# Attention walks of a graph network: the next chunk's small products a quarter chunk earlier, and the gathers' waits at the beginnings of the groups

## The reference, cut to what matters

```python
h = einsum(x, W)                        # per node, 8 heads
e = leaky_relu(a_src[src] + a_dst[dst], 0.2)
e_max = segment_max(e, dst)             # over the edges of a destination
e_exp = exp(e - e_max[dst])
out = segment_sum(h[src] * e_exp, dst) / segment_sum(e_exp, dst)
```

## Time and profile before

| | |
|---|---|
| median of three runs | 6823.27 us |
| profiled execution: its time | 6820.69 us |
| profiled execution: its span | 6818.9 us |
| TensorE matmul / weight load busy | 4848.6 us (71%) / 3393.1 us (50%) |
| VectorE, ScalarE, GpSimd busy | 3942.6 us (58%), 2371.9 us (35%), 3022.1 us (44%) |
| granted TensorE clock, mean | 0.808 |
| messages L903 (all four walks) | 416 instructions of about 1247 ns |
| gathers L780 (all four walks) | 1664 instructions of about 0.98 us |

### The profile page before, as it was taken

How to read it: one execution, slowest core, us unless ns; L and a number is a source line. 1 busy time by engine, 2 the same in 40 slices (tenths; PEclk the granted TensorE clock), 3 DMA queues, 4 the chain that set the end, 5 groups by cost and what they waited for, 6 DMA issues and landing times. The chain is left out here.

```text
span 6818.9 us, 79751 instructions
## 1 busy us (share of the span) xinstructions
PE 4848.6 (71%) x19231; PEld 3393.1 (50%) x19232; DVE 3942.6 (58%) x8585; ACT 2371.9 (35%) x5719; POOL 3022.1 (44%) x2932
## 2 busy tenths in 40 slices
PE   2777659537775937776577738888899555477999
PEld 2455436325553725544355534444587333355777
DVE  4566733446667246665466657666424788787333
ACT  1343312124443224443244424544221122275333
POOL 2666432446662046662666536666000677553000
PEclk8777859767887968887688858888899665687999
DMA  4455424234442034443444511111001899873000
GB/s 117 151 167 166 106 66 127 86 103 143 152 153 61 1 105 152 143 152 90 144 142 152 133 41 29 31 31 26 21 9 51 315 379 381 295 220 118 10 14 23
DMA packets 543457, 819.09 MB, mean 120 GB/s; under 512 B 87966, under 2 KB 421967, under 8 KB 542839
## 3 DMA queue, kind: packets, MB, share of 16 engines
q1 hardware_dynamic: 396388, 432.93, 19.6%
q0 software_dynamic: 140832, 376.78, 19.3%
q10 hardware_dynamic: 5907, 5.92, 0.3%
HBM read 658.06 MB, written 157.71 MB: 120 GB/s over the span
## 5 line engine op out<-in xcount | busy, mean ns | idle before, releaser
L780 POOL DMA_INDIRECT l_edges_stage<-l_h_rows,src_t x832 | 822.6, 989 | 592.7 <-issue 222.5
L2507 POOL DMA_INDIRECT l_edge_kv<-l_kv_rows,src_t x416 | 477.0, 1147 | 651.1 <-POOLq L2414 517.5
L1093 PE MATMUL l_edges_ps_sum<-l_edges_msg,l_edges_hot 128*128 128x264 f32 x1664 | 591.0, 499 | 213.4 <-DVE l_attn_acc L922 134.1
L2935 POOL DMA_INDIRECT l_gate_edges_srow<-l_gate_src_rows,l_gate_edges_idx x512 | 487.1, 951 | 325.7 <-issue 140.8
L2560 PE MATMUL l_edge_ps_q<-l_q_q,l_edge_hot 128*128 x832 | 352.5, 598 | 287.6 <-issue 201.7
L3071 PE MATMUL l_gate_edges_ps<-l_gate_edges_wide,l_gate_edges_hot_lo 128*128 128x500 f32 x1024 | 492.8, 627 | 83.3 <-issue 57.3
L780 POOL DMA_INDIRECT l2a_edges_stage<-l2a_h_rows,src_t x416 | 408.2, 981 | 295.6 <-issue 126.5
L1093 PEld LDWEIGHTS l_edges_ps_sum<-l_edges_msg,l_edges_hot 128*128 128x128 f32 x1664 | 357.6, 239 | 362.9 <-DVE l_attn_acc L922 207.8
L780 POOL DMA_INDIRECT l2b_edges_stage<-l2b_h_rows,src_t x416 | 408.6, 982 | 288.6 <-issue 126.2
L2560 PEld LDWEIGHTS l_edge_ps_q<-l_q_q,l_edge_hot 128*128 128x128 f32 x832 | 238.4, 300 | 401.8 <-issue 353.9
L922 DVE TENSOR_TENSOR l_attn_acc<-l_attn_acc,l_edges_ps_sum 128x264 f32 x832 | 349.8, 420 | 84.5 <-DVE l_attn_acc L922 20.3
(11 more groups left out here) (784 smaller groups left out, 10870.1 us busy)
## 6 DMA issues: line engine op xcount, KB each, us to landing
l_edge_e<-e_rows SPq DMA_DIRECT2D x416, 128.0 KB
l_val_rows<-l_edge_vj SPq DMA_DIRECT2D x104, 512.0 KB
l_agg_stage<-l_val_rows SPq DMA_DIRECT2D x52, 1024.0 KB, 5.5
l_edges_rel_b<-rel_rows SPq DMA_DIRECT2D x52, 512.0 KB
l_edges_ea<-in_edge_attr SPq DMA_DIRECT2D x48, 512.0 KB
e_rows<-l_edges_e_s SPq DMA_DIRECT2D x48, 512.0 KB
l_experts_w<-in_L_ffn_w SPq DMA_DIRECT2D x32, 512.0 KB, 5.0
l_gate_edges_lo_b<-l_gate_edges_lo_rows SPq DMA_DIRECT2D x64, 256.0 KB
```

Source lines behind the costliest of these rows:

```text
L780: nc.gpsimd.indirect_dma_start(out=stage[:, c % SL, u, :], out_offset=None, in_=h_rows, in_offset=bass.IndirectOffsetOnAxis(ap=K.src_t[:, ...
L1093: nc.tensor.matmul(ps_sum[u][:], hot[:, g, u, :], msg[:, g % 2, u, :], start=True, stop=True).then_inc(summed, 1)
L2507: nc.gpsimd.indirect_dma_start(out=kv[:, m, u, :], out_offset=None, in_=kv_rows, in_offset=bass.IndirectOffsetOnAxis(ap=K.src_t[:, n * EB ...
L2935: nc.gpsimd.indirect_dma_start(out=srow[:, n % 4, u, :], out_offset=None, in_=src_rows, in_offset=bass.IndirectOffsetOnAxis(ap=idx[:, n * ...
```

## The change

On VectorE the chain of the next chunk starts before the first message: `rescale`, `logits`, `weigh` 0, `tile_ends` with no adds in it, `weigh` 1, `tile_tops` with the adds of group 0, `weigh` 2, `edge_maxima` with the adds of group 1, `weigh` 3, the adds of group 2, `exponents`, `nodes_hot`, the adds of group 3. TensorE's small products each move ahead by one `scatter`, ScalarE's `rescaling` moves to behind group 1, and GpSimd waits for the small products at the beginnings of the groups, beside the wait for the message. Nothing is computed otherwise.

```diff
@@ gpsimd
                         if c >= SL:
                             pool.wait_ge(msg_built, NG4 * (c - SL) + g + 1)
+                            signal = (lg_turned, ends_placed, inits_made, max_turned)[g]
+                            pool.wait_ge(signal, c - SL + 2)
                         for u in range(g * GR, (g + 1) * GR):
-                            if c >= SL and u % GR == GR // 2:
-                                signal = (lg_turned, ends_placed, inits_made, max_turned)[g]
-                                pool.wait_ge(signal, c - SL + 2)
@@ vector, chunk(c, j, i, after)
-                    weigh(c, i, 0)
                     blks = block_ids(nc, mybir.EngineType.DVE, K, c)
                     rescale(c, blks[0])
                     if after >= 1:
                         logits(c + 1, j, i + 1)
-                    for g, step in enumerate((tile_ends, tile_tops, edge_maxima)):
+                    weigh(c, i, 0)
+                    if after >= 1:
+                        tile_ends(c + 1, i + 1, lambda u: None)
+                    for g, step in ((0, tile_tops), (1, edge_maxima)):
                         weigh(c, i, g + 1)
                         if after >= 1:
                             step(c + 1, i + 1, adds(c, g, blks))
...
+                    weigh(c, i, 3)
+                    for u in range(GR):
+                        adds(c, 2, blks)(u)
                     if after >= 1:
                         exponents(c + 1, i + 1)
                     if after >= 2:
                         nodes_hot(c + 2, j, i + 2)
                     for u in range(GR):
-                        adds(c, GR - 1, blks)(u)
+                        adds(c, 3, blks)(u)
@@ scalar, chunk
                         last_maxima(c, m, g)
+                        if after and g == 1:
+                            rescaling(c + 1, 1 - m)
...
                     if after:
-                        rescaling(c + 1, 1 - m)
                         edges_hot(c + 1, 0)
@@ tensor, chunk
+                    if after >= 1:
+                        turn_logits(c + 1, 1 - m)
                     scatter(c, 0)
                     if after >= 1:
-                        turn_logits(c + 1, 1 - m)
+                        place_ends(c + 1)
                     if after >= 2:
                         turn_attr(c, m, 0, j * 16 + 16 * (m + 1))
                     scatter(c, 1)
                     if after >= 1:
-                        place_ends(c + 1)
+                        place_tops(c + 1)
                     if after >= 2:
                         attr_terms(c, 0)
                     scatter(c, 2)
                     if after >= 1:
-                        place_tops(c + 1)
+                        place_f(c + 1)
+                        turn_maxima(c + 1)
                     if after >= 2:
                         turn_attr(c, m, 1, None)
-                    scatter(c, 3, 0, GR // 2)
-                    if after >= 1:
-                        place_f(c + 1)
-                        turn_maxima(c + 1)
-                    scatter(c, 3, GR // 2)
+                    scatter(c, 3)
```

More of the change, by code:

```diff
@@ L1107, in chunk @@
                     if after >= 1:
-                        place_tops(c + 1)
+                        place_f(c + 1)
+                        turn_maxima(c + 1)
                     if after >= 2:
                         turn_attr(c, m, 1, None)
-                    scatter(c, 3, 0, GR // 2)
-                    if after >= 1:
-                        place_f(c + 1)
-                        turn_maxima(c + 1)
-                    scatter(c, 3, GR // 2)
+                    scatter(c, 3)
                     if after >= 2:
                         blks = block_ids(nc, mybir.EngineType.PE, K, c + 2)
-                    if after >= 2:
                         attr_terms(c, 1)
```

## The result

The changed kernel takes **7072.4 us** (median of 4 runs, 7061.9 to 7079.0), the kernel before 6824.3 on the same chip: ratio **1.036** (95% interval 1.035 to 1.038). The forecast was 6890, the range 6740 to 6990. The direction was right; the loss is 248 us and not 70. The profiled execution took 7067.5 us, its span is 7065.6.

The account below looks back on a forecast made before the run. A ring through GpSimd was taken as the bound, `place_tops` and `expand` showing only after GpSimd pauses. Terms gave +0.60 us a chunk, +55 us in 92 chunks, plus 11 and 4: 6820.7 + 70 = 6890 us, range 6740 to 6990.

Parts of the forecast that it names:

- rival A: TensorE's old order, not gathers, delays `place_tops` and `expand`; in the new order both show when they end: 6620 us, chance 0.10.
- (a): GpSimd's wait at group 0: restart 2.64 us behind the reduction, now also needing message 0; +0.70 us a chunk.
- (b): GpSimd's wait at group 1: `ends_placed` is there in time, the stop of 0.52 us goes; -0.30 us a chunk.
- (c): GpSimd's wait for the message of group 0, 0.68 us in some chunks, joins the group 0 wait; -0.15 us a chunk.
- (d): GpSimd's wait at group 2: `place_tops` ends before the stop but is held as before; +0.25 us a chunk.
- (e): Way from `inits_made` to `expand`, with one more `scatter` and a message: late by 0 to 2.3 us, taken as +0.10 a chunk.
- Rival D: TensorE becomes late, its clock at 0.50 from `inits_made` to `expand`: 6988 us, chance 0.13.
- (f): GpSimd's wait for `max_turned` at group 3: there 4.1 to 5.2 us after `inits_made`, needed after 5.3; costs nothing.
- (g): VectorE's turn of the loop: the load of block numbers now in the open before `rescale`; +0.9 us in 12 chunks, +11 us.
- (h): Last chunks of a walk, without gathers: the load of block numbers in the open, +1 us each, +4 us in all.
- B: Results are held, but not longer than some 3 us, so `place_tops` comes out by itself: 6775 us, chance 0.16.
- C: The change doesn't move the chain, since `logits` waits for `expanded` before and after: 6823 us, chance 0.17.

Follow-up runs that it names:

- no_pacing_b2: Kernel before with GpSimd's waits for the four small products left out, so it waits for messages alone; on a chip with late TensorE results: ratio 1.083.
- half_rows: Kernel before with gathers of half a row from the fourth chunk of each walk on, as many instructions: ratio 0.999.
- on_expanded_u1: Kernel before with GpSimd's stop at u = 2 waiting for `expanded` instead of `lg_turned`, and moved to u = 1: ratio 0.996, 6801 us beside 6822.
- pool_only: Kernel before with only GpSimd's waits for the small products moved to the groups' beginnings, old orders kept; on the 6174 chip: ratio 0.999.
- pool_only_2: Kernel before with only GpSimd's waits moved to the groups' beginnings, old orders kept, repeated on a chip with late TensorE results: ratio 1.017.
- pool_swap: Kernel before with GpSimd's waits at the groups' beginnings, the wait for the small product put ahead of the wait for the message: ratio 1.002.
- after_swap: Changed kernel with GpSimd's two waits of groups 1 to 3 swapped, those at group 0 left: ratio 1.041 to the kernel before.
- ids_early: Changed kernel with TensorE's load of block numbers ahead of `scatter` 3 instead of behind it: ratio 1.040 to the kernel before.
- order_only: Changed kernel with GpSimd's waits for the small products back in the middle of the groups; on the 6174 chip: ratio 1.055 to the kernel before.

## Why the prediction was right or wrong

**The frame** (a ring through GpSimd, results out behind its stops) stood. Its picture of the hold was too narrow: I tied it to `place_tops` and `expand`, on the ground that `turn_maxima` showed at once. That one ended early in a run; the other two end 7 to 10 us into one, or behind a stop too short to let anything out. no_pacing_b2, half_rows and on_expanded_u1 show the rest. The page "SBUF — State Buffer" of the Trainium skill (section "Who interferes with whom") says of the ports of the memory that TensorE and ScalarE wait for nobody. The late results don't refute that: TensorE itself may well run on, and what is late is that others see its results. That the rule makes them show at once, as rival A took it, holds on the 6174 chip (pool_only: 0.04 us) and not with holds (1.4 us behind the stop).

**(a)** right: 2.64 us from the reduction to the restart, forecast 2.64. **(b)** right, -0.29. **(c)** it went into (a), as said.

**(d)** right in size (+0.16 for +0.25), not in cause: the hold is hardly longer (1.49 us behind the stop for 1.39), the restart behind `inits_made` is 0.5 us dearer by the double wait, and in 20 of the 92 chunks the stop moves to u = 12. I had not priced the second wait at all: pool_only_2 against pool_swap makes it 1.5% of the time in the old order. In the new one the message is the last at u = 0, so at most half of that applies, and after_swap shows that taking it away gives nothing back there.

**(e)** is the step that failed first. From `inits_made` to `expand` I had 10.4 to 13.5 us, and two rows give both ends: 3023.57 to 3033.68 and 2996.15 (copy L878 of the chunk before) to 3009.57. But I took +0.10, almost the short end, because "one overlap is gained, as the load of block numbers runs under `scatter` 3". That is the step that failed: the load does start under `scatter` 3, but it lasts about 3 us in more than half of the chunks, of which 2.56 us are idle in the rows above, and the way is 12.2 us in the mean. `expand` ends 1.3 us behind the stop on the average (-1.0 to +3.7 in l2a) and shows 1.96 behind it, where the sum had 1.1. So +0.86 us for +0.10. **Rival D** named a late TensorE and its 6988 us came nearest, but by luck: it asked for a clock at 0.50 on this way, and the clock was 0.84 in the mean, with the short and the long way above at 0.83 and 0.87. To shorten the way doesn't help either: ids_early ended `expand` 1.5 us sooner and it showed 0.2 sooner, because the hold is behind it. The held sums of `scatter` 3 keep VectorE's adds, load and rescaling behind the stop as well, which I had called covered by the wait for `expanded`.

**(f)** failed: 1.10 us and not 0.30 at u = 12, +0.80. The sum 4.1 to 5.2 against 5.3 us was right for a result that shows when it ends (`turn_maxima` ends at 3028.69, and GpSimd asks for it at 3029.03). I had put the term at nothing and not asked what happens when the stop at u = 8 falls away. Where `place_tops` shows at once, the run isn't broken at u = 8, and `turn_maxima` ends 8 us or more into it. That is so in all 16 chunks in which GpSimd's gap of 1.6 us at u = 1 breaks the run early.

**(g)** The cover of the turn went, not only that of the load: in before `expand` showed 5 us ahead of GpSimd's stop in those chunks and the stop was no longer for it (2.1 us). The chunk behind a turn and the next are together 4.8 us longer than two others, for 2.8 before: +2.0 us a turn against the 0.9 that I added. The two chunks around a turn last 7 us longer than two others (60.6 for 53.9); the rest of that is the chunk ahead with its gap and its stop at u = 12. **(h)** +33 us for +4: the last but one chunk lasts 27.9 to 29.1 us for 22.4. It is the one with GpSimd's chunk 25 beside it, with the same gap and the same stop.

Of the 178 us missing, (e) and (f), 0.76 and 0.80 us a chunk above the forecast, make 144 in 92 chunks. The stretches between and behind the walks, for which I had nothing, are 23 more in the two profiled executions, and single executions of the changed kernel differ by up to 17. The rest is small and isn't split further: the gap at u = 1 (+0.23), (g) and (h), which in part count the same chunks as (f), on one side, and the gathers, shorter by 0.37 us a chunk, on the other. **Rivals A and B** are excluded with holds; on the 6174 chip A's premise is true, yet order_only was slower there by 5.5%, for A took GpSimd's 20 us as the bound and overlooked that the new order's chain is itself about 24 us (TensorE's load of block numbers lasts about 3 us in it). **C** is excluded by the interval.

Open: why results are held and why at one time or chip and not at another; what makes the gap at u = 1 and the long load of block numbers; what the changed kernel takes on the 6174 chip.

## What to carry to other kernels

Before moving a wait, ask what it does besides waiting: here a stop of the issuing engine lets another engine's results out, and the length of the run between two stops of 1 us or more, not the number of stops, is what costs. A stop that is taken away comes back at the next result that ends late in the now longer run, so sum over all stops of the ring, not over the one that goes. When a term has two ends that rows bear out and the cover is about as long as the near end, take the middle. And look up how long a hidden load lasts before counting its cover as gained.

## What the runs showed of the hardware

- Beside most of the runs, results that TensorE ends 8 us or more into an unbroken run of indirect gathers are mostly held: they are seen 0.7 to 3 us behind GpSimd's last gather, in no_pacing_b2 up to 9.8 us late. Updates of VectorE and ScalarE aren't held (0 of 2728). In the four runs on the 6174 chip nothing was, and the kernel before is 10% faster there (6174 against 6822 to 6877 us).
- A stop of GpSimd of less than 1.0 us doesn't end such a hold (56 of 56 small products held behind one in the kernel before), a longer one does (0 of 183 held).
- Halving the gathers' bytes changes nothing in that (0.999).
- GpSimd starts a gather 0.27 us behind a wait that the gather carries, 0.78 behind one that stands alone ahead of it.
- A load of 16 block numbers into TensorE's registers lasts 1.1 us without gathers beside it, 1.8 in most chunks of the kernel before, and up to 3 us and more in the changed kernel.
